# A corner table with two pixels a row instead of four, in a deformable convolution

## The reference

```
py, px = base + off                        # one pair for each pixel and tap
v00, v01 = gather(y0, x0), gather(y0, x0 + 1)
v10, v11 = gather(y0 + 1, x0), gather(y0 + 1, x0 + 1)
s = v00*(1-wy)*(1-wx) + v01*(1-wy)*wx + v10*wy*(1-wx) + v11*wy*wx
out = einsum('bckhw,ock->bohw', s * 2*sigmoid(mod), reg_w)
```

## Time and profile before

| | |
|---|---|
| runs, us | 6361.84, 6363.08, 6366.41 (median 6363.08) |
| profiled execution: span, us | 6362.2 |
| PE, DVE, POOL, ACT busy | 82%, 76%, 62%, 41% |
| DMA queue 0 (POOL), queue 1 (SP), queue 10 (ACT), share of 16 engines | 56.6%, 14.1%, 1.1% |

### The profile page before, as it was taken

The page is one execution under the profiler, slowest core; times in us unless marked ns, Lnnn a source line. Parts: engine busy times, 40 slices in busy tenths (PEclk is TensorE's granted clock), DMA queues, the critical chain, the costliest instruction groups (busy, mean ns, idle before and its releaser), DMA issues. The chain is left out here.

```text
span 6362.2 us, 66252 instructions
## 1 busy us (share of the span) xinstructions
PE 5196.9 (82%) x16608; PEld 2627.8 (41%) x16608; DVE 4850.7 (76%) x6696; ACT 2639.4 (41%) x6416; POOL 3950.9 (62%) x4386
## 2 busy tenths in 40 slices
PE   5987878888887888888787878886666759999998
PEld 4432333333332333333233333322222327777777
DVE  3898888888788888878788888878777464666664
ACT  1343434343333333333333333333333643666663
POOL 3777777777777777777777777777777002222221
PEclk9999999999999999999999989998888879999999
DMA  7787877777777777777777777777777864555555
GB/s 242 219 243 222 249 224 239 228 222 221 224 227 218 225 223 219 223 222 220 226 216 228 214 232 209 230 209 229 211 220 219 301 234 130 148 149 147 151 151 180
DMA packets 583162, 1359.23 MB, mean 214 GB/s; under 512 B 96744, under 2 KB 262508, under 8 KB 581480
## 3 DMA queue, kind: packets, MB, share of 16 engines
q0 software_dynamic: 329216, 1045.50, 56.6%
q1 hardware_dynamic: 225624, 287.23, 14.1%
q10 hardware_dynamic: 28048, 23.40, 1.1%
HBM read 1240.28 MB, written 115.46 MB: 213 GB/s over the span
## 5 line engine op out<-in xcount | busy, mean ns | idle before, releaser
L510 POOL DMA_INDIRECT G<-table,om x3840 | 3660.3, 953 | 1202.2 <-issue 1157.8
L667 DVE TENSOR_TENSOR G<-G,ps_w 128x1536 f32<-128x1536 f32 x960 | 1681.2, 1751 | 502.1 <-DMA G<-table,om 486.0
L792 PE MATMUL ps_y<-sT,R 128*128 128x512 f32 x3840 | 2028.7, 656 | 26.7 <-ACT yb L558 26.7
L542 ACT ACTIVATE ps_a<-G,om 128x128 f32<-128x128 f32 x3840 | 1192.7, 357 | 1873.6 <-DMA G<-table,om 1229.3
L780 PE MATMUL ps_t<-ident,acc 128*128 128x128 f32 x3840 | 665.0, 299 | 940.2 <-DVE acc L678 915.4
L780 PEld LDWEIGHTS ps_t<-ident,acc 128*128 128x128 f32 x3840 | 434.8, 147 | 1693.5 <-DVE acc L678 1587.1
L550 ACT ACTIVATE sT<-ps_t 128x512 f32<-128x512 f32 x960 | 572.1, 596 | 1080.9 <-PE ps_y L792 1079.3
L792 PEld LDWEIGHTS ps_y<-sT,R 128*128 128x128 f32 x3840 | 726.8, 210 | 601.6 <-issue 601.5
L1588 DVE TENSOR_TENSOR vl<-ps_v,vh 128x512 fp32r<-128x512 f32 x1024 | 657.0, 686 | 335.4 <-ACT vh L1537 335.4
L1522 POOL DMA_DIRECT2D ut<-spec_dram x512 | 262.5, 513 | 854.1 <-PE ps_v L1603 639.3
L671 DVE TENSOR_TENSOR ps_a<-G,ps_a 128x512 f32<-128x512 f32 x960 | 668.3, 696 | 128.6 <-ACT ps_a L542 29.1
(11 more groups left out here) (186 smaller groups left out, 2394.8 us busy)
## 6 DMA issues: line engine op xcount, KB each, us to landing
tt<-kern_dram SPq DMA_DIRECT2D x512, 192.0 KB, 3.4
G<-table,om POOLq DMA_INDIRECT x3840, 3.7
y_dram<-yb SPq DMA_DIRECT2D x64, 512.0 KB, 4.8
yin<-y_dram SPq DMA_DIRECT2D x16, 2048.0 KB, 13.0
ut<-spec_dram POOLq DMA_DIRECT2D x256, 96.0 KB, 3.4
spec_dram<-spec_hi SPq DMA_DIRECT2D x64, 256.0 KB, 2.6
ut<-spec_dram POOLq DMA_DIRECT2D x256, 48.0 KB, 3.0
om_dram<-om_next SPq DMA_DIRECT2D x60, 150.0 KB, 3.4
```

Source lines behind the costliest of these rows:

```text
L510: pool.indirect_dma_start(G[k % RING][:, j, :], None, tables[g // GI], bass.IndirectOffsetOnAxis(ap=om[g % 2][:, j, 0, k:k + 1].bitcast(I3 ...
L542: last = nc.scalar.activation(ps_a[:, j, :], G[k % RING][:, j, 0:C], ACT.Copy, scale=om[g % 2][:, j, 1, k:k + 1])
L667: nc.vector.tensor_tensor(three, three, ps_w[:, :, h:h + 1].to_broadcast([128, 12, C]) .rearrange("p (j c) d -> p j c d", j=4), ALU.mult). ...
L792: last = nc.tensor.matmul(ps_y[:, half, :], R[:, k, 128 * half:128 * half + 128], sT[n % 2][:, :], start=(k == t0), stop=(k == ends[br] - 1))
```

## The change

A row of the table now holds two corners, the pixel and the one below it, 1 KB. The two corners to the right are the next row of the table, so a gather still fetches 2 KB into the same tile, beginning at row index x 1 KB and reaching over two neighbouring rows. One row is added at the end for the last pixel. The tile is written twice and not four times, and the corners arrive in the order 00, 10, 01, 11, so two weight planes change places.

```diff
@@ stage_normalise
         def write_table(q, i, half):
             src = xt[i][64 * half:64 * half + 64, :, :]
-            for slot, (dy, dx) in enumerate(((0, 0), (0, 1), (1, 0), (1, 1))):
+            for dy in range(2):
                 y0 = 8 * i + half + 2 - dy
-                dst = grid[y0:y0 + 7:2, 2 - dx:2 - dx + W, slot * C:(slot + 1) * C]
+                dst = grid[y0:y0 + 7:2, 2:2 + W, dy * C:(dy + 1) * C]
                 q.dma_start(dst.rearrange("t x c -> x t c"), src).then_inc(table_written, 16)
...
-            for slot in range(4):
-                dy, dx = divmod(slot, 2)
-                zero_rows(slot, 0, 2 - dy)
-                zero_rows(slot, TS - 1 - dy, TS)
+            pool.dma_start(tables[0][TROWS:TROWS + 1, :], zero[0:1, :]).then_inc(border_written, 16)
+            for dy in range(2):
+                zero_rows(dy, 0, 2 - dy)
+                zero_rows(dy, TS - 1 - dy, TS)
...
-            for slot in range(4):
-                dy, dx = divmod(slot, 2)
-                zero_columns(slot, dy, 0, 2 - dx)
-                zero_columns(slot, dy, TS - 1 - dx, TS)
+            for dy in range(2):
+                zero_columns(dy, 0, 2)
+                zero_columns(dy, TS - 1, TS)
...
-            sp.wait_ge(table_written, 16 * 8 * GI)
+            sp.wait_ge(table_written, 16 * 4 * GI)
@@ stage_branches
             def write_table(c):
                 sp.wait_ge(xn_ready, c + 1)
                 for half in range(2):
-                    for slot, (dy, dx) in enumerate(((0, 0), (0, 1), (1, 0), (1, 1))):
+                    for dy in range(2):
                         y0 = 8 * c + half + 2 - dy
-                        dst = far[y0:y0 + 7:2, 2 - dx:2 - dx + W, slot * C:(slot + 1) * C]
+                        dst = far[y0:y0 + 7:2, 2:2 + W, dy * C:(dy + 1) * C]
...
             for y in (0, TS - 2):
                 sp.dma_start(far[y:y + 2, :, :].rearrange("y x s -> (y x s)").rearrange("(p n) -> p n", p=TS),
-                             zeros[0:TS, :]).then_inc(far_written, 16)
+                             zeros[0:TS, 0:4 * C]).then_inc(far_written, 16)
...
+            sp.dma_start(tables[1][TROWS:TROWS + 1, :], zeros[0:1, 0:2 * C]).then_inc(far_written, 16)
...
                 for r in range(2):
-                    last = nc.vector.tensor_tensor(plane(m, 2 + 2 * r), a[:, r, :], fr[:, 1, :], ALU.mult)
+                    last = nc.vector.tensor_tensor(plane(m, 3 + r), a[:, r, :], fr[:, 1, :], ALU.mult)
                 st.then(last)
                 for r in range(2):
-                    last = nc.vector.tensor_tensor(plane(m, 1 + 2 * r), a[:, r, :], plane(m, 2 + 2 * r), ALU.subtract)
+                    last = nc.vector.tensor_tensor(plane(m, 1 + r), a[:, r, :], plane(m, 3 + r), ALU.subtract)
@@ program
-        tables = [nc.dram_tensor(f"table{b}", (TROWS, 4 * C), F32, kind="Internal").ap() for b in range(B)]
+        tables = [nc.dram_tensor(f"table{b}", (TROWS + 1, 2 * C), F32, kind="Internal").ap() for b in range(B)]
```

## The result

The changed kernel takes 6342.08 us, the median of 6 runs (6338.16 to 6346.6); the kernel before took 6362.69 beside it, the median of 6 (6359.0 to 6366.41). The ratio is 0.9967, with a 95% interval of 0.9956 to 0.9978: 20.6 us less, and beyond the 0.2% that the prediction took for no change. The forecast was 6344.6 in a range of 6337 to 6356.

What follows compares the result with a forecast made beforehand. POOL's fixed pace of gathers bounds the loop; stage_normalise ahead of it is bound by DMA and the PE chain. Only that stage shrinks: 6362.2 - 18.5 = 6343.7, with 0.9 for the median 6344.6 us, range 6337 to 6356.

Steps and rivals of the forecast that it cites:

- Step 1: In stage_normalise, 64 table writes of batch 0 become 32, freeing 16.7 us of DMA engine time.
- Step 2: In stage_normalise, batch 0's border zeros go from 16 DMAs to 9 with half the bytes, freeing 2.3 us.
- Step 3: Table writes and borders of batch 0 together: 19.0 us of engine time, so last writes land 20.3 us earlier.
- Step 4: ACT's copies and PE's first window convolution in stage_normalise come 16.8 to 23.9 us earlier; 18.5 taken for the stage.
- Step 5: Head of stage_branches, 80 to 143 us: SP's halved zeros for batch 1 are already covered, gain 0.
- Step 6: In the gather loop, batch 1's table writes on SP fall from 64 to 32: gain 0, outer bound 12 us.
- Steps 7 and 8: Gathers with overlapping 2 KB reads at 1 KB steps, and two swapped weight planes, cost the same: 0.
- Step 9: Everything after the gather loop, 1418 us, is untouched: 0.
- A: Rival, 17%: wom's load in ACT's queue, not table writes, holds tile 1's copy; only 12.9 us gained, 6350.2.
- B: Rival, 6%: each gather index costs POOL two read descriptors; 2610 to 3640 us slower, time 8950 to 9980.
- C: Rival, 4%: the gathers' overlapping reads crowd one part of memory; at double transfer time, 2050 us slower.
- D: Rival, 3%: POOL's 12 us of small waits also go, with the PE chain's optimistic 23.9: 6327.

Runs made afterwards that it cites:

- e10: The changed kernel with all gathers after the first 24 fetching 1 KB for an index instead of 2 KB: 6339.21 us, ratio 0.9964.
- e3: The changed kernel with each table write of batch 0 issued a second time, into a spare table: 6359.15 us, ratio 0.9991.
- e4: The changed kernel run once more, unaltered: 6345.52 us, ratio 0.9968.
- e6: The changed kernel with POOL's zeros of batch 0 written a second time, into a spare table: 6356.95 us, ratio 0.9975.
- e5: The kernel before with the same zeros cut otherwise, POOL's 67 partitions into 64 and 3, SP's of batch 1 also recut: 6344.06 us, ratio 0.9960.
- e7: The changed kernel with all 32 table writes of batch 0 issued by SP, none by ACT: 6352.13 us, ratio 0.9969.
- e1: The changed kernel with the change kept for batch 0's table only, batch 1's as before: 6348.08 us, ratio 0.9972.
- e2: The changed kernel with the change kept for batch 1's table only, batch 0's as before: 6364.54 us, ratio 0.9999.
- e9: The changed kernel with POOL's zeros cut into 64 and 3 partitions and SP's zeros recut too: 6320.5 us, ratio 0.9937.
- e13: The changed kernel with only POOL's zero rows of batch 0 cut into 64 and 3 partitions: 6318.85 us, ratio 0.9933.
- e11: The kernel before with all zeros cut otherwise, the same kernel as e5 run again: 6338.28 us, ratio 0.9960.
- e8: The kernel of e7 with PE also computing the second window convolution in stage_normalise: 6353.91 us against the kernel before, ratio 0.9972.

## Why the prediction was right, and where it was not

- *What bounds the kernel.* Right. POOL's 953 ns and the gap of 0.30 us stayed, and what got shorter is stage_normalise. e10 shows that transfers in the loop cost nothing.
- *Step 1, table writes of batch 0, 16.7 us of the engines' 47.* By e3 they are worth 12.7 us (14.3 against e4), where 16.7 at 93.9% busy would be 17.8: too high by 3 to 5.
- *Step 2, borders of batch 0, 2.3 us.* This is the term that was mis-sized: it measured 5.5 (e6) to 8.0 (e3). The step took the share of queue 0, which is an average over 16 engines, and halved it. e5 shows that zeros of the same size cost 9.4 us more or less by the way they are cut.
- *Step 3, 20.3 us.* 20.7, but because the two errors cancel (12.7 + 8.0 for 17.8 + 2.5), and that is luck.
- *Step 4, the PE chain, 18.5 between 16.8 and 23.9.* Copy 5 was to come at 41.2 and came at 40.06, the convolution near 44 and came at 43.41. The prediction took a value between the chain's 16.8 and the DMA's 20.3; the convolution ends 2.2 us ahead of the next stage. e7, where the convolution starts 7 us earlier and the stage still ends within what the changed kernel does by itself, shows that it is the DMA that sets it, by little.
- *Step 5, the head, 0.* Wrong: 5.7 us. "SP comes out of them at 112.96 ... 11 us of cover" took the end of SP's instructions for the end of the transfer. The rest of the zeros runs on for microseconds on one engine, and the loading of R and the first gathers come late with it: 3 us, by e1 against e2. That they queue on that engine is argued from the rates; that the zeros are the cause is shown by e1, e2 and e5. The other 2.6 us are the second convolution, 15.61 to 13.01. In before the granted clock had fallen during it and after the change it had not (the windows of 5 us in it; the columns are busy times of PE, PEld, DVE, ACT and POOL, then clock, DMA share, GB/s):

```profile
82.00:87.00 5.00, 5.00 (x24) 5.00 (x23) 2.86 (x14) 0.06 (x1) 1.03 (x1) 0.53 0.85 366
```

```profile
62.00:67.00 5.00, 5.00 (x41) 5.00 (x40) 2.25 (x11) 0.00 (x0) 1.73 (x2) 1.00 1.04 452
```

0.53 is near the lower of the two levels (1.2 of 2.4 GHz) and 1.00 is the upper. PE had stood idle 3.9 us ahead of it in before and 3.3 us in after. It takes 13.01 us in after, e4 and e10, and 14.47 to 15.98 in the others, among them e1, e6, e9 and e13, whose pause is 3.3 us as well. The rows show one difference: the first convolution, ahead of that pause, took 13.8 to 14.0 us in the three and 14.5 to 15.0 in these four. What decides stays open, so these 2.6 us came with the changed kernel in both its profiles and in e10, but no run ties them to a part of the change.
- *Step 6, table writes of batch 1, 0.* Right: e2 is at 0.9999. POOL's waits for acc fell from 18.7 to 13.7 us, 3.1 of it by the one of 6.7 that became 3.6, which is step 5's.
- *Steps 7 and 8, gathers and weights, 0.* Right: 953 ns, 71.0%.
- *Step 9, the tail, 0.* 3 us longer, within what it does by itself: from 1418.0 in e5 to 1425.3 in e11, which are the same kernel.
- *Rivals.* A fell with the copy of tile 1 at 18.83; e3, where it goes back to 32.37, shows the table writes as the cause. B fell with 953 ns and C with 71.0%. Of D, the stage gave 20.7 and not 23.9, and the small waits mostly stayed (12.0 to 10.1 us).

The sum was 18.5 + 0 and came out at 20.6 between medians and 24.4 between profiles: the mechanism is the one forecast. The stage gave 2.2 us more than the forecast and the head 5.7, and in the profiles the tail took 3.0 back. That the median came within 2.5 us of 6344.6 is thus in part luck, in step 3 and in the tail.

## What to carry to other kernels

Where a stage is bound by DMA, a queue's share of the engines is no price: rows of zeros on 67 partitions cost 9.4 us more than the same bytes on 64 and 3, though the share called all zeros 4.7 us. Try another cut of a transfer whose partitions don't divide evenly. The end of a DMA's issue is not the end of its transfer; cover that is read from the issuing engine's timeline must be read again in the DMA lines (here, tenths at 0 or 1 with a steady 25 GB/s were one engine at work). Fewer bytes pay only where bytes bound: halving them ahead of the loop was worth 20 us, halving them within it nothing.

## What the hardware showed unexpectedly

- The POOL time of one and the same indirect DMA differs between kernels and stays the same all through an execution: a median of 953 or 954 ns in nine profiles, 946 to 948 in e5, e11, e9 and e13, and 957 in e8. Over 3840 gathers that is 10 to 21 us less, or 10 us more. e13 ties it to cutting four of POOL's DMAs of zeros, which are issued in the first 20 us. No run says whether it is their number, their shape or the place of POOL's instructions that counts, and e8, whose POOL does the same as that of e7 (953 ns), is longer. e5 and e11, the same kernel, also differ by 9 us in it. The mechanism is open.
- A gather of 128 indices takes 953 ns at 1 KB for an index as at 2 KB (e10), and at a source step of 1 KB with overlapping reads as at 2 KB without.
- The same 98 matmuls took 13.01 to 15.98 us after a pause of 3.3 to 8 us; where the clock was read in 5 us of them, it was 1.00 in the first case (after) and 0.53 in a long one (before, 15.61 us). A pause of 3.3 us came with both lengths.
